# A conv-attention and expert hybrid: one batch's input and the bias tables in the setup, and the order of ScalarE and TensorE in the last passes

## The chip, the cores and the metric

The kernel runs on one core of one Trainium2 chip. A core has TensorE (PE, matrix products into PSUM), VectorE (DVE), ScalarE (ACT), GpSimd (POOL) and SyncE (SP, which here only issues DMAs). Each engine works through its own instruction stream in order, and streams meet at semaphores. The metric is the device time of one execution in microseconds, median of several runs.

## What is computed

The input x has 16 batches of 16 x 48 tokens of 128 channels. Three blocks follow one another, each added to its input:

```python
x = x + conv_attention(group_norm(x))     # 8 heads, softmax over 768 tokens of a batch, two relative-position biases
t = tokens(x)
t = t + additive_attention(layer_norm(t))
#   hidden = tanh(A[:, :, None, :] + B[:, None, :, :]);  logits = hidden . w2;  attn = softmax(logits);  attn @ v
t = t + experts(layer_norm(t))            # softmax gate, top 2 of 8 experts, capacity 1920 rows each,
                                          # gelu(rows @ w1 + b1) @ w2 + b2, weighted and added back
```

The additive attention needs a tanh for every query, key and hidden unit, and the biases of the first attention are gathered from two small tables (95 x 8 and 31 x 8).

## The kernel before

Work is a pipeline over batches with five stages: `pre` (group norm, q, k, v, and q and k split into three bf16 parts), `max` (row maxima of the scores), `mid` (the first attention and what `add` needs), `add` (the tanh attention) and `end` (gate, top 2, and rows sent to the experts). In pass b, `pre` works on batch b + 3, `max` on b + 2, `mid` on b + 1, `add` on b and `end` on b - 1. A pass has 24 ticks, and a tick has four slots. Tables (`AT`, `MAX_COUNTS`) say at which tick a product stands, and every engine writes the same passes in its own stream, so the order is fixed when the program is written.

**The setup.** `passes` (L189 on, in the listing below) starts with pieces of passes: `pre` of batch 0, ticks 0 to 17; then each engine's `prepare`; then `pre` of batch 1, ticks 0 to 17; then batch 0's last `pre` ticks with the first maxima, then `max` of batch 0, and so on. SP loads the x of batch 0, weights and tables, then writes two constant blocks into `q_max` and two into `k_max` (L620 to L624; the latter wait for ScalarE's `setup_act`), stores batch 0's parts (L693) and loads them back for the maxima (`load_max`, which waits for `parts_stored`). Batch 1's x is loaded at the first tick of its pass (L688), into `x_in`. That tile also holds the rest of k of batch 0 while it is split (`qk_rest`, L265). DVE's `prepare` first makes the bias tables: seven small operations that split the table `tn_raw` into three bf16 parts and put them together in `tn_all` (L1141 to L1155), then eight copies that spread it into `bias_q` (L1157). It goes on with transposed weights (L1164 to L1177) and gate constants. ScalarE fills the other 48 partitions of `bias_q` behind that (L858). The first scores of batch 0 (L948) read `bias_q`. GpSimd's `prepare` makes masks and ends with a DMA that clears expert rows (L789).

**The last passes.** Pass 15 is the one with `add` but no `mid`: per tick GpSimd writes three sums into one of four `hidden` slots (L803, 3 instructions), ScalarE takes the tanh of these in place, 128 x 2304 elements, the wide one (L902), then a narrow one for the fourth column straight from `b_rep` (L906); TensorE multiplies the slot by w2 into `logits` (L978, the product of tick t stands in tick t + 1). Every fourth tick a block of 128 queries is complete: DVE takes its maximum (L1447, L1449), ScalarE its exponential (L886, `exp_logits`, at t = 5, 9, 13, 17, 21 ahead of that tick's wide tanh, and for the last block at t = 1 of the next pass), TensorE transposes it and multiplies by v (L1071, L1074), and DVE normalises and adds. The first product of the next block waits for the exponential, since it overwrites `logits`. GpSimd may run four ticks ahead of the products. Pass 16 has `end` alone: the last block, layer norm, gate (L1078), top 2, positions (L1083 to L1094), then twelve row sends by GpSimd (L814).

**The experts.** Ten chunks of 384 rows per pair of experts: transposes (L458), up products (L471), gelu (L510), down products (L482), weights by DVE (L545 to L552), and three scattering DMAs a chunk by GpSimd (L583). The first up product waits for rows, weights and the bias `down_b`.

## Time and profile before

| | |
|---|---|
| median of 3 runs | 2384.56 us (2372.84 to 2385.24) |
| profiled execution, its own time | 2384.78 us |
| its span, first to last instruction | 2383.0 us |
| PE busy | 2053.2 us (86%) |
| DVE, ACT, POOL busy | 1675.7 (70%), 1683.2 (71%), 1461.3 us (61%) |
| mean granted TensorE clock | 0.951 |

Time and span differ by 1.8 us, which lies around the first and last instruction. Busy shares are means over a setup, twelve equal passes in a loop, some unrolled ones and the expert part, so what a stage waits for has to be read from that stage. In the page's 40 slices of 60 us, PE is busy for 2 tenths in the first, and for 7, 7, 5 and 4 tenths in the four slices from 1966 to 2145 us; elsewhere it is at 7 to 9 tenths or more. A granted clock of 1.00 is 2.4 GHz and one of 0.50 is 1.2 GHz.

### The profile page before, as it was taken

The numbers are of one execution on the slowest core, as the hardware profiler recorded it, in microseconds if no ns is written. First come the engines' busy times: TensorE is split into PE (matmuls) and PEld (weight loads), VectorE is DVE, ScalarE is ACT, GpSimd is POOL, SyncE is SP. The second block draws the span as 40 slices with busy tenths as digits, with TensorE's granted clock in tenths as the row PEclk, the third lists the DMA queues.
The fourth block names the chain that finished last, engine by engine and source line by source line (L and its number), as shares of the span: only waits on it lengthen the run. The fifth ranks groups of instructions, "written<-read, shape, count | busy, mean of one in ns | idle before, by whom it ended". The sixth has DMA issues, their size and how long they took to land.

```text
span 2383.0 us, 56242 instructions
## 1 busy us (share of the span) xinstructions
PE 2053.2 (86%) x17665; PEld 1122.5 (47%) x17665; DVE 1675.7 (70%) x4534; ACT 1683.2 (71%) x1933; POOL 1461.3 (61%) x1525
## 2 busy tenths in 40 slices
PE   2889999989998999989998999999999977549986
PEld 1344444444444444444444444444444433338775
DVE  5787787787878787868786878787877665324433
ACT  5238787877887788778787878788878977613332
POOL 3006576656666656565666666666657877627777
PEclk7799999999999999999999999999999988869998
DMA  4546322322222223222323131313131000025553
GB/s 94 89 86 128 95 48 61 55 62 56 61 56 61 56 59 57 58 60 51 66 50 68 42 70 29 81 32 77 32 65 32 12 6 4 7 54 90 84 86 37
DMA packets 157499, 137.99 MB, mean 58 GB/s; under 512 B 24665, under 2 KB 149814, under 8 KB 157104
## 3 DMA queue, kind: packets, MB, share of 16 engines
q1 hardware_dynamic: 119376, 109.87, 22.5%
q0 software_dynamic: 23824, 16.85, 5.2%
q10 hardware_dynamic: 13968, 7.30, 1.2%
q8 instruction: 154, 2.52, 0.5%
q14 instruction: 177, 1.45, 0.2%
HBM read 82.68 MB, written 54.52 MB: 58 GB/s over the span
## 4 chain that ended last, share of the span: by engine, by line
PE 39%; DVE 22%; issue 13%; DVEq 9%; POOL 6%; ACT 4%; POOLq 3%; DMA 2%; SPq 0%; another core or an unknown queue 0%; ACTq 0%
PE logits L978 12%; DVE max_halves L1261 4%; POOL out_dram L583 4%; PE ring L1052 3%; PE av_bank L964 3%; POOLq L802 3%; PE ring L1074 3%; PE ring L1066 3%; PE scores L948 3%; PE scores L951 2%; ACT hidden L902 2%; DVE logit_bias L1447 2%; POOL hidden L803 2%; PE ring L1071 2%; DVEq L1448 2%
## 5 line engine op out<-in xcount | busy, mean ns | idle before, releaser
L803 POOL TENSOR_SCALAR hidden<-b_rep,a_cols 128x768 f32<-128x768 f32 x1152 | 1057.1, 920 | 765.6 <-issue 302.9
L902 ACT ACTIVATE hidden<-hidden 128x2304 f32<-128x2304 f32 x384 | 816.1, 2125 | 16.4 <-POOL hidden L803 16.4
L978 PE MATMUL logits<-hidden,w_shifted 128*32 128x384 f32 x6144 | 591.6, 504 | 65.3 <-ACT hidden L906 30.9
L879 ACT ACTIVATE probs<-scores 128x512 f32<-128x512 f32 (+1 forms) x768 | 391.9, 545 | 325.6 <-PE scores L951 320.9
L1261 DVE TENSOR_REDUCE max_halves<-ring 128x1 f32<-128x384 f32 (+4 forms) x896 | 471.3, 550 | 115.8 <-PE ring L1052 114.2
L906 ACT ACTIVATE hidden<-b_rep,a_cols 128x768 f32<-128x768 f32 x384 | 358.4, 933 | 0.0
L1052 PE MATMUL ring<-k_max,q_max 112*128 112x384 bf16 (+4 forms) x1024 | 296.0, 319 | 34.8 <-DVE max_halves L1261 25.9
L978 PEld LDWEIGHTS logits<-hidden,w_shifted 128*32 128x32 f32 x6144 | 164.0, 110 | 314.9 <-issue 246.7
L948 PE MATMUL scores<-bias_q,onehot_k 112*128 112x512 bf16 (+1 forms) x768 | 276.4, 360 | 4.8 <-ACT probs L879 1.8
L951 PE MATMUL scores<-q_parts,k_parts 98*128 98x256 bf16 (+1 forms) x1536 | 277.3, 262 | 0.0
L814 POOL DMA_INDIRECT expert_rows<-rows,slots x198 | 199.5, 1007 | 64.2 <-issue 32.7
L964 PE MATMUL av_bank<-probs,v_aug 128*32 128x256 f32 (+1 forms) x3072 | 224.8, 364 | 6.3 <-DVE headsT_raw L1433 6.1
L951 PEld LDWEIGHTS scores<-q_parts,k_parts 98*128 98x128 bf16 x1536 | 153.3, 100 | 116.8 <-issue 20.1
L1052 PEld LDWEIGHTS ring<-k_max,q_max 112*128 112x128 bf16 x1024 | 91.0, 99 | 245.2 <-issue 95.0
L886 ACT ACTIVATE probs<-logits,logit_bias 128x768 f32<-128x768 f32 x96 | 86.6, 902 | 132.7 <-DVE logit_bias L1449 127.9
L1074 PE MATMUL ring<-v,probs1T 128*128 128x128 f32 x1152 | 153.2, 284 | 21.8 <-DVE max_halves L1261 13.0
L1074 PEld LDWEIGHTS ring<-v,probs1T 128*128 128x128 f32 x1152 | 139.5, 195 | 41.4 <-DVE max_halves L1261 19.7
L510 ACT ACTIVATE hidden<-scores,eb1T 128x384 f32<-128x384 f32 x80 | 46.2, 581 | 132.2 <-PE scores L471 129.6
L1319 DVE COPY probs1T<-ring 128x384 f32<-128x384 f32 x192 | 102.6, 548 | 34.5 <-PE ring L1071 34.2
L964 PEld LDWEIGHTS av_bank<-probs,v_aug 128*32 128x32 f32 x3072 | 70.3, 109 | 103.8 <-issue 80.8
L482 PEld LDWEIGHTS logits<-probs,hidden 128*128 128x128 f32 x960 | 113.4, 192 | 12.1 <-issue 1.7
L482 PE MATMUL logits<-probs,hidden 128*128 128x128 f32 x960 | 113.7, 275 | 1.6 <-DVE gn_small L552 1.6
(262 smaller groups left out, 2585.8 us busy)
## 6 DMA issues: line engine op xcount, KB each, us to landing
qk_parts<-qk_parts_sb SPq DMA_DIRECT2D x16, 1152.0 KB, 4.7
q_parts<-qk_parts SPq DMA_DIRECT2D x192, 96.0 KB, 3.2
k_parts<-qk_parts SPq DMA_DIRECT2D x192, 96.0 KB, 4.3
q_max<-qk_parts SPq DMA_DIRECT2D x96, 96.0 KB
k_max<-qk_parts SPq DMA_DIRECT2D x96, 96.0 KB
expert_rows<-clear_row ACTq DMA_DIRECT2D x9, 792.0 KB, 5.0
x_in<-in_x_dram SPq DMA_DIRECT2D x96, 64.0 KB
x<-in_x_dram SPq DMA_DIRECT2D x96, 64.0 KB
```

The lines of the kernel that those rows point to most:

```text
L482: last = mm(logits[:, n % 2, P * b_:P * b_ + P], gelu_out[n % 2][:, j, P * b_:P * b_ + P], down_w[r][:, j, :], start=(j == 0), stop=(j == 3))
L803: last = g.tensor_scalar(hidden[:, q % SLOTS, o, :], b_rep[:, side], 1.0, a_cols[:, side, a_col(q, o):a_col(q, o) + 1], ALU.mult, ALU.add)
L879: s.activation(probs0[:, d % 3, 2 * pair:2 * pair + 2, 0:n_], scores[:, pair].rearrange("p (j l) -> p j l", j=2)[:, :, 0:n_], ACT.Exp) \
L902: s.activation(hidden[:, t % SLOTS, 0:3, :], hidden[:, t % SLOTS, 0:3, :], ACT.Tanh)
L906: s.activation(hidden[:, t % SLOTS, 3, :], b_rep[:, side], ACT.Tanh, bias=a_cols[:, side, col:col + 1]).then_inc(tanh_done, 1)
L948: mm(bank[:, :, 0:n_], onehot_k[:], bias_q[:, h:h + 2, q0 - P * kb:q0 - P * kb + n_], start=True, stop=False, skip_group_check=True)
L951: last = mm(bank[:, j, 0:n_], k_parts[0:98, h + j, P * kb:P * kb + P], q_parts[0:98, h + j, q0:q0 + n_], start=False, stop=True, skip_grou ...
L964: last = mm(av_bank[32 * g:32 * g + 32, q0 - lo:q0 - lo + n_], v_aug[:, side, kb, 4 * quad + g, :], probs0[:, d % 3, g, 0:n_], start=(kb = ...
L978: last = mm(logits[32 * g:32 * g + 32, half, 0:HALF], w2_shifted[:, k, :], hidden[:, q % SLOTS, g, HALF * half:HALF * half + HALF], start= ...
L1052: last = mm(bank[:, keys * j:keys * j + keys], q_max[:, h + j, P * qb:P * qb + P], k_max[:, h + j, lo:lo + keys], start=True, stop=True)
L1074: last = mm(bank[:, 0:P], probs1T[:, P * kb:P * kb + P], v1[:, ps.side(stage), kb, :], start=(kb == 0), stop=(kb == TB - 1))
L1261: v.tensor_reduce(max_halves[:, h:h + n_, part], bank[:, 0:n_ * keys].rearrange("p (h k) -> p h k", h=n_), AX.X, ALU.max, negate=True).the ...
```

## The change

- SP loads the x of batch 1 in the setup, behind the weights, once TensorE has finished transposing batch 0's x (`ring_filled` at 2). The rest of k of batch 0 goes to `x2` instead of `x_in`. Batch 0's parts are stored ahead of the two `k_max` copies, which now stand in `copy_tables`.
- The bias tables (split, put together, and the copies into partitions 0 to 63 of `bias_q`) move from DVE's `prepare` to the end of GpSimd's `prepare`, behind its clearing DMA, with a semaphore `bias_made` for ScalarE and TensorE. There are nine small operations instead of seven.
- In pass 15 `exp_logits` stands between the wide and the narrow tanh.
- `keep_warm(n)` issues n products of 112 x 512 bf16 into `scores[:, 0]`, which nobody reads: 3 in each of the 24 ticks of pass 15, and 14, 4, 16 and 90 of them in ticks 3, 7, 8 and 12 of pass 16.
- In pass 16 ScalarE computes one Gelu of one column behind the gate's exponential.

```diff
+WARM_AT = {3: 14, 7: 4, 8: 16, 12: 90}
...
-        qk_rest = [xT[:], x_in[:].rearrange("p b c -> p (b c)")]
+        def qk_rest(w, c):
+            if w == 0:
+                return xT[:]
+            return (x_in if positive(c) else x2)[:].rearrange("p b c -> p (b c)")
...
+            sp.wait_ge(ring_filled, 2)
+            load_x(1)
             sp.wait_ge(made, 3)
             sp.dma_start(q_max[48:96, :, :], hot_t.unsqueeze(1).to_broadcast([48, H, L])).then_inc(copies_in, 16)
             sp.dma_start(q_max[96:112, :, :], hot_n.unsqueeze(1).to_broadcast([16, H, L])).then_inc(copies_in, 16)
-            sp.wait_ge(setup_act, 1)
-            sp.dma_start(k_max[48:96, :, :], ct_wide).then_inc(copies_in, 16)
-            sp.dma_start(k_max[96:112, :, :], cn_wide).then_inc(copies_in, 16)
...
-                        if t == 0 and positive(count := c * 2):
+                        if t == 0 and positive(count := c * 2) and positive(c - 1):
...
                             if not positive(c):
+                                copy_tables()
                                 load_max(c, 0)
...
                 pool.dma_start(cleared[0], clear_source).then_inc(rows_sent, 16)
+                g.tensor_copy(tn_hi, tn_raw)
+                pool.drain()
+                g.tensor_tensor(tn_rest, tn_raw, tn_hi, ALU.subtract)
+                pool.drain()
...
+                g.memset(flag[:, 0:1], 0.0).then_inc(bias_made, 1)
+                for h in range(H):
+                    last = g.tensor_copy(bias_q[0:64, h, :].rearrange("p (b n t) -> p b n t", n=16, t=8),
+                                         tn_all[0:64, :].rearrange("p (w h) -> p w h", h=H)[:, :, h][:, ::-1]
+                                         .rearrange("p (b t) -> p b t", t=8).unsqueeze(2).to_broadcast([64, TB, 16, 8]))
+                last.then_inc(bias_made, 1)
...
-            act.wait_ge(setup_dve, 2)
+            act.wait_ge(bias_made, 1)
...
-                    if ps.has("add") and t >= 5 and t % 4 == 1:
+                    if ps.has("add") and ps.has("mid") and t >= 5 and t % 4 == 1:
                         exp_logits(ps.batch("add"), t // 4 - 1)
...
                         s.activation(hidden[:, t % SLOTS, 0:3, :], hidden[:, t % SLOTS, 0:3, :], ACT.Tanh)
+                        if not ps.has("mid") and t >= 5 and t % 4 == 1:
+                            exp_logits(b, t // 4 - 1)
...
+                        if not ps.has("add"):
+                            s.activation(logit_bias[:, 0:1], ident[:, 0:1], ACT.Gelu)
...
+                    pe.wait_ge(bias_made, 2)
                     pe.wait_ge(setup_act, 2)
...
+            def keep_warm(n):
+                for _ in range(n):
+                    mm(scores[:, 0, :], ones_bf[0:112, :], bias_q[:, 0, 0:512], start=True, stop=True)
...
+                        if slot == 2 and ps.has("add") and not ps.has("mid"):
+                            keep_warm(3)
+                        if slot == 3 and not ps.has("add") and ps.has("end") and not positive(NB - ps.b):
+                            if t in WARM_AT:
+                                keep_warm(WARM_AT[t])
```

DVE's `prepare` loses the matching lines (L1141 to L1160 before), and the waits on `setup_dve` are renumbered.

GpSimd at the end of its setup, before and after. Names in a row are out<-in, with the shape of the output.

```order
L786 MEMSET rows 128x792
L725 MEMSET flag 128x1
L789 DMA expert_rows<-clear_row 128x12x132
L803 TENSOR_SCALAR hidden<-b_rep,a_cols 128x768 x72
```

```order
L801 DMA expert_rows<-clear_row 128x12x132
L802 CAST tn_parts<-hidden 112x384
L804 TENSOR_TENSOR hidden<-hidden,tn_parts 112x384
L806 CAST tn_parts<-hidden 112x384
L808 TENSOR_TENSOR tn_parts<-hidden,tn_parts 112x384
L811 TENSOR_SCALAR tn_parts<-tn_parts,part_mask 112x384 x3
L813 TENSOR_TENSOR tn_parts<-tn_parts 112x384
L815 TENSOR_TENSOR tn_parts<-tn_parts 112x384
L817 MEMSET flag 128x1
L819 COPY bias_q<-tn_parts 64x768 x8
L836 TENSOR_SCALAR hidden<-b_rep,a_cols 128x768 x72
```

Seventeen operations that stood on DVE between the split of batch 0 and the transposed weights now stand behind GpSimd's clearing DMA.

SP's DMAs from the last small weights to the load of batch 0's parts, before and after.

```order
L620 DMA q_max<-k_parts 48x8x768
L621 DMA q_max<-k_parts 16x8x768
L623 DMA k_max<-q_parts 48x6144
L624 DMA k_max<-q_parts 16x6144
L693 DMA qk_parts<-qk_parts_sb 128x2x2304
L640 DMA q_max<-qk_parts 16x4x768 x3
L640 DMA k_max<-qk_parts 16x4x768 x3
L597 DMA x_in<-in_x_dram 128x1x128 x6
```

```order
L603 DMA x_in<-in_x_dram 128x1x128 x6
L628 DMA q_max<-k_parts 48x8x768
L629 DMA q_max<-k_parts 16x8x768
L704 DMA qk_parts<-qk_parts_sb 128x2x2304
L635 DMA k_max<-q_parts 48x6144
L636 DMA k_max<-q_parts 16x6144
L651 DMA q_max<-qk_parts 16x4x768 x3
L651 DMA k_max<-qk_parts 16x4x768 x3
```

The six loads of x move from behind the load of the parts to the front, and the store of the parts moves ahead of the `k_max` copies.

TensorE in pass 16, from the last block to the first expert rows, before and after.

```order
L1074 MATMUL ring<-v,probs1T 128x128 x6
L1037 MATMUL ring<-ident,rows 128x128 x6
L1078 MATMUL ring<-gateT,headsT 128x8 x6
L1083 MATMUL ring<-chosen,before_same 128x48
...
L1094 MATMUL ring<-chosen,ones_bf 128x8 x6
L458 MATMUL av_bank<-ident,xT 128x128 x3
```

```order
L1116 MATMUL ring<-v,probs1T 128x128 x6
L1022 MATMUL scores<-bias_q,ones_bf 128x512 x14
L1079 MATMUL ring<-ident,rows 128x128 x6
L1022 MATMUL scores<-bias_q,ones_bf 128x512 x4
L1120 MATMUL ring<-gateT,headsT 128x8 x6
L1022 MATMUL scores<-bias_q,ones_bf 128x512 x16
L1125 MATMUL ring<-chosen,before_same 128x48
...
L1136 MATMUL ring<-chosen,ones_bf 128x8 x6
L1022 MATMUL scores<-bias_q,ones_bf 128x512 x90
L464 MATMUL av_bank<-ident,xT 128x128 x3
```

The extra products stand in TensorE's stream behind the last block, the transposes, the gate and the positions, the 90 directly ahead of the first expert rows.

## Rows read from the trace of the kernel before

**Rows 1.** Stretches by time: start:end, length, busy us (count) per engine, PEclk, DMA

```profile
40.00:60.00 20.00, 3.91 (x14) 3.07 (x14) 5.55 (x28) 4.33 (x2) 0.00 (x0) 0.50 0.38 84
```

**Rows 2.** Timeline of DVE in the setup: start, us, operation, [idle before <-releaser]

```profile
28.37 0.77 DVE L1142 CAST tn_parts<-hidden 112x384 bf16<-112x384 f32 x1
...
38.85 0.29 DVE L1164 COPY wv1T<-logits 128x128 f32<-128x128 f32 x1
...
54.02 0.56 DVE L1229 COPY xT<-ring 128x384 f32<-128x384 f32 x1 [10.66 <-PE ring L1037]
```

**Rows 3.** Timeline of SP's DMA issues in the setup

```profile
33.12 1.84 SPq L693 DMA_DIRECT2D qk_parts<-qk_parts_sb  x1
...
47.61 3.81 SPq L597 DMA_DIRECT2D x_in<-in_x_dram  x6
```

**Rows 4.** Timeline of DVE where GpSimd works too

```profile
14.55 0.17 DVE L1131 TENSOR_TENSOR ln_small<-ln_small 128x7 f32<-128x7 f32 x1
14.79 1.41 DVE L1133 SCALAR_TENSOR_TENSOR ln_small<-ln_small 128x7 f32<-128x7 f32 x1
...
2004.38 0.81 DVE L1133 SCALAR_TENSOR_TENSOR ln_small<-ln_small 128x7 f32<-128x7 f32 x1
```

**Rows 5.** Timeline of POOL: what its instructions take

```profile
14.72 1.54 POOL L719 TENSOR_SCALAR_AFFINE_SELECT k_parts<-k_parts 48x768 bf16<-48x768 bf16 x1 [0.19 <-issue]
16.45 1.92 POOL L719 TENSOR_SCALAR_AFFINE_SELECT k_parts<-k_parts 16x768 bf16<-16x768 bf16 x1 [0.19 <-issue]
...
29.90 1.26 POOL L789 DMA_DIRECT2D expert_rows<-clear_row  x1 [0.72 <-POOL flag L725]
...
2000.54 13.44 POOL L803 TENSOR_SCALAR hidden<-b_rep,a_cols 128x768 f32<-128x768 f32 x15
```

**Rows 6.** Timeline of PE at the first scores of batch 0

```profile
91.96 0.63 PE L951 MATMUL scores<-q_parts,k_parts 98*128 98x256 bf16 x2
92.39 0.63 PE L948 MATMUL scores<-bias_q,onehot_k 112*128 112x512 bf16 x1
```

**Rows 7.** Timeline of ACT in pass 15, and the page's group of the wide tanh

```profile
1999.49 0.90 ACT L886 ACTIVATE probs<-logits,logit_bias 128x768 f32<-128x768 f32 x1 [1.05 <-DVE logit_bias L1449]
...
2018.07 0.90 ACT L886 ACTIVATE probs<-logits,logit_bias 128x768 f32<-128x768 f32 x1 [6.16 <-DVE logit_bias L1449]
...
2032.09 0.90 ACT L886 ACTIVATE probs<-logits,logit_bias 128x768 f32<-128x768 f32 x1 [1.54 <-DVE logit_bias L1449]
...
2044.68 0.90 ACT L886 ACTIVATE probs<-logits,logit_bias 128x768 f32<-128x768 f32 x1 [0.24 <-DVE logit_bias L1449]
...
L902 ACT ACTIVATE hidden<-hidden 128x2304 f32<-128x2304 f32 x384 | 816.1, 2125 | 16.4 <-POOL hidden L803 16.4
```

**Rows 8.** Timeline of PE from pass 15 to the first expert chunk

```profile
2011.55 2.93 PE L1074 MATMUL ring<-v,probs1T 128*128 128x128 f32 x12 [3.77 <-DVE probs1T L1319]
...
2016.71 1.50 PE L1078 MATMUL ring<-gateT,headsT 128*128 128x8 f32 x12
...
2026.98 1.60 PE L1074 MATMUL ring<-v,probs1T 128*128 128x128 f32 x12 [0.56 <-DVE probs1T L1319]
...
2088.04 1.54 PE L1037 MATMUL ring<-ident,rows 128*128 128x128 f32 x6 [5.71 <-DVE rows L1217]
2090.23 2.73 PE L1078 MATMUL ring<-gateT,headsT 128*128 128x8 f32 x12 [0.65 <-DVE headsT L1291]
...
2121.32 0.90 PE L458 MATMUL av_bank<-ident,xT 128*128 128x128 f32 x3 [22.59 <-DMA xT<-expert_rows]
...
2124.64 2.93 PE L471 MATMUL scores<-probs1T,probs 128*128 128x384 f32 x4 [0.82 <-DMA v<-in_L_ffn_b_dram]
...
2130.57 1.48 PE L471 MATMUL scores<-probs1T,probs 128*128 128x384 f32 x4
```

**Rows 9.** Timeline of DVE at the end of pass 15

```profile
2073.67 0.16 DVE L1321 RECIPROCAL row_scale<-row_sum 128x1 f32<-128x1 f32 x1 [8.81 <-remote]
```

**Rows 10.** Stretches by time in the last passes, columns as in rows 1

```profile
2072.00:2074.00 2.00, 0.00 (x0) 0.00 (x0) 0.26 (x2) 0.00 (x0) 0.00 (x0) 0.65 0.01 0
```

51 lines of the change are left out of this document (24 added, 27 removed).

## The prediction

> **What bounds the kernel now.** I read the 40 slices first, then stretches and the timeline of each engine where a slice is thin. The change touches nothing in the loop over the full passes, which is most of the span, so its worth lies in two places: the first 95 us and the last 400.
>
> In the setup between 40 and 60 us nothing is near busy: PE has 3.91 us of work in 20, DVE 5.55, POOL none, and the granted clock is at its lower level, 0.50 [rows 1]. DVE shows why. It is through with batch 0 at 28.37, spends 10.48 us on the bias tables (28.37 to 38.85), ends its preparation and then sits idle for 10.66 us until PE has transposed the x of batch 1, so that x enters DVE at 54.02 [rows 2]. That x was issued only at 47.61 [rows 3], behind a DMA queue that had waited for the store of batch 0's parts. From 54.02 on the chain goes through DVE and PE without such a gap up to the maxima of batch 0 and the first scores, at about 92 [rows 6], so what starts this chain earlier moves the rest of the kernel.
>
> In pass 15 the longest stream is ScalarE's: 24 ticks of a wide tanh of 2.1 us [rows 7] and a narrow one. It is interrupted at the exponentials, which wait for DVE's maximum of the block: 1.05, 6.16, 1.54 and 0.24 us before four of them, and the fifth is like the fourth [rows 7]. Behind it comes a sequential tail: last block, layer norm, gate, sends, first chunk. There PE runs at the lower level: the same gate product takes 2.73 us where it takes 1.50 elsewhere, the value product 2.93 against 1.60, and an up product pair 2.93 against 1.48 [rows 8].
>
> **The change part by part.**
>
> *DVE's preparation and the early x: 21.1 us.* The tables leave DVE: 10.48 us off its path. The next thing that was late is x. SP reaches the new load at about 21 us, when its small weights are issued; six loads take 3.81 us to issue [rows 3], and PE had them 5.5 us after the first issue (47.61 to 53.10, which is 54.02 less the transposes). So x is there at about 27, while DVE and PE are ready at 32. The idle 10.66 us goes as well, whole. 10.48 + 10.66 = 21.1 us: x enters DVE at 32.9 instead of 54.02. The two `q_max` copies behind the load on SP come 3.8 us later, and the `k_max` copies behind the parts; only the maxima wait for them. The store of the parts moves from 33.12 [rows 3] to 28.5, DVE's end of batch 0; at the 11.7 us that it and what shared the queues took before (33.12 to 44.8) the load of the parts starts at 40.2 and, with 2.8 us of issue and about 5 of landing, is there at 48. The first maximum, at 68.5 before, wants it at 47.4 if all 21.1 us are kept, so this costs 0.5 us at most and nothing if the next term is real.
>
> *GpSimd's tables in DVE's way: +7 us.* The tables now run on GpSimd from 31.2 (29.90 + 1.26 [rows 5]), just when DVE does the group norm of batch 1. A DVE instruction with two operands in SBUF that takes 0.17 us took 1.41 us when a GpSimd selection of 1.54 us had begun 0.07 us before it, and such instructions take 0.81 us in a row under GpSimd's sums, one per sum [rows 4, 5]. So a DVE instruction of this kind waits for the GpSimd instruction under way. GpSimd's price: a sum of 768 elements takes 13.44 / 15 = 0.90 us, a selection of as many 1.54 to 1.92 [rows 5]. The nine small operations have 384 elements, so 0.45 to 0.96 each; at 0.6, with seven drains of 0.19, the table is ready at 31.2 + 6.7 = 37.9. Each of the eight copies reads and writes 768: 0.90 to 1.92; I take 1.1, near the sum, since a copy is plain arithmetic too, but its source is read backwards in steps. DVE reaches its first two-operand instruction 3.1 us after x enters, at 36.1, and has some twelve until the normalised x is out (two of the mean, one of the variance, nine of the root), 0.245 us apart when alone. Two of GpSimd's small operations and eight copies are still to come then, and each lets one DVE instruction through: 2 x (0.6 - 0.25) + 8 x (1.1 - 0.25) = 7.5; I take 7, since a few overlap reads from PSUM. The bounds are nothing, if these copies do not block, and 2 x 0.7 + 8 x (1.92 - 0.25) = 14.8 us. The SBUF page of the Trainium skill ("SBUF — State Buffer", section "Who interferes with whom") states the same as an exclusive lock: a DVE instruction with two SBUF inputs contends with a GpSimd one that reads SBUF, and the second to issue fully blocks. By that rule this part of the change is charged as here, and without it the sum below would be 7 us lower.
>
> The other waits on the tables have room: ScalarE's part of `bias_q` and its constant rows take 11.3 us behind 37.9, and the first scores would come at 92 - 14 = 78.
>
> *The exponential behind the wide tanh: -5.1 us.* The wait now runs beside 2.1 us of tanh (about 2.0 from start to start). Gain per block: the wait, at most 2.0. 1.05 + 2.0 + 1.54 + 0.24 + 0.25 = 5.1. What is queued behind the exponential is the narrow tanh, 0.8 us, which ends when it ended before. The first product of the next block, which waits for the exponential, comes up to 2.0 us later in its tick, and through it GpSimd's sums four ticks on: product 1.5 us, sums 3 x 0.90, a send of 1.0 where there is one, so 5.2 us, against 0.8 + 2 x 2.85 = 6.5 until ScalarE wants them. That holds with 1.3 us to spare. Bounds: 0, if that loop closes, and 5.1 + 4.1 (the rest of the 6.16) if DVE's chain also shortens.
>
> *Fillers in pass 15: -1.4 us.* A product of 512 columns takes 0.43 us at the lower clock level (two halves, 91.96 to 92.39 [rows 6]), so 0.22 at the upper. Three are 0.65 us a tick, less than PE's idle 1.25 before most products. With the clock up, the value product ahead of the longest wait takes 1.6 instead of 2.9 us [rows 8], on the path to the 2018.07 exponential: 1.3, taken as 1.4 with the products around it. Bounds: +3 (five block ends pushed by 0.65) and -3.
>
> *Fillers in pass 16: -1.7 us.* The transposes at 2088.04 go from 1.54 to 0.87 and the gate from 2.73 to 1.50, together 1.9; the four fillers between them, 0.9 us, stand in a gap of 0.65 [rows 8] and give 0.2 back. The 14 (3.0 us at full speed, 6.0 at half) fit in the idle 5.71 ahead of the transposes, about even in the worst case; the 16 (3.5) in the 5.0 ahead of the positions. Nothing warms PE while it waits for the last exponential, so the last block stays at the lower level.
>
> *The 90, and the first chunk: -2.9 us.* They stand in the 22.59 us in which PE waits for rows [rows 8]: 90 x 0.215 = 19.4 us at full speed. PE is then idle for 3.2 us. After idling from 2068.7 the clock was still granted whole until 2072 and fell in the stretch behind it, 0.65 [rows 10], so it should just last. The first up products start with the bias DMA as before, but take 2 x 1.45 less (2.93 to 1.48 [rows 8], for two pairs). The Gelu table, 1.3 us of ScalarE, is off the path too, but gelu kept up anyway: nothing for it. GpSimd's scatters, the bound of the expert part, start 2.9 earlier.
>
> The sum: 2384.8 (the profiled execution, 0.2 above the median) - 21.1 + 7 - 5.1 - 1.4 - 1.7 - 2.9 = 2359.6, **2360 us**.
>
> One piece stays unexplained: 8.81 us in which DVE stands before a reciprocal although its product was done [rows 9]. I leave it in; were it chance, the time falls by up to 8.8 in either kernel, and one run of before was 12 us below the others.
>
> **The rivals.**
>
> *No contention.* GpSimd's copies don't hold DVE up, or are done before it comes. For: DVE's casts and copies beside GpSimd's masks in the setup are not slowed. Against: rows 4. Time: 2359.6 - 7 + 0.5 = 2353.
>
> *Strided reads cost GpSimd more.* A copy takes 1.92 like the dearest selection: contention 14.8, time 2384.8 - 21.1 + 14.8 - 11.1 = 2367. For: the source steps by 16 bytes. "GPSIMD Engine Reference" of the Trainium skill, section "Performance pitfalls for Q7 kernels", has a rule for custom kernels that reads with more than 8 bytes a step cost half as much again; 1.35 a copy would be an estimate from it, and 2362.
>
> *The 90 fillers become the wait.* If PE does not come to full speed under them they take 90 x 0.43 = 38.7 us, 16 more than the gap of 22.6. The rows come through with PE late, the up products start some 15 later, and terms of the fillers are lost: 2384.8 - 21.1 + 7 - 5.1 + 15 = 2381. Against: dense up products brought the clock up within 6 us at 2124 to 2131 [rows 8]. If it rises after that time, the loss is only about 3.
>
> *Slower than before.* GpSimd's broadcast copy, reversed and in steps, is far dearer than any row shows. It decides at the eight copies in the setup: each costs DVE D - 0.25, and the other terms with the small operations give 31.5, so the point is D = 4.2 us a copy. At 5 us: 2384.8 - 31.5 + 38 = 2391. No row comes to half of that.
>
> *The tail does not move.* The block ends turn out to wait on something that follows along (GpSimd's sums or DVE's chain), and only the setup pays: 2384.8 - 14.1 = 2371.
>
> **How the numbers follow.** Chances: forecast 0.48 (2352 to 2366 around it), no contention 0.16, strided reads 0.13, the tail does not move 0.10, fillers late 0.08, slower 0.05. A measurement of this kernel can tell about 0.5% from no change, 12 us. Faster by over 0.5% (below 2372.6) are the forecast, the first two rivals and 0.06 of the tail case: 0.83. Within 0.5% are the rest of the tail case and the late fillers: 0.12. Slower: 0.05. The unexplained 8.8 us is no case of its own and only widens the lower end. For 8 in 10 the range reaches from 2345 (no contention and half of the 8.8) to 2375.
>
> **What the profile would show.** x of batch 1 enters DVE at about 33 and the first scores come at 78; DVE's small two-operand instructions between 36 and 47 last about as long as GpSimd's copies; GpSimd's copies take 0.9 to 1.9 us; no wait above 0.1 before the exponentials but the second; PEclk 1.00 through pass 15; the 90 fillers end before the rows arrive, and the first up products take 1.5 a pair. Wrong would be a first score before 73 or after 84, a copy above 2 us, a new wait of ScalarE for sums, or PE still in fillers when the rows are there.

## The result and the profile after

The changed kernel takes 2396.11 us (median of 16 runs, 2383.59 to 2406.66), the kernel before 2384.65 us (16 runs of the same set). The ratio is 1.0052 with a 95% interval of 1.0032 to 1.0071: 12 us slower, where the prediction had 25 us faster. By the rule that sorts runs into fast and slow, one run of e5 below (3305.97 us at a granted clock of 0.555) and six of the 13 of e1 (2398.34 to 2412.35 us, clocks of 0.940 to 0.949) are slow; without those six e1's median is 2387.05 us, so e1 alone is weak evidence. The profiled execution took 2394.67 us, its span is 2392.9 us and its mean granted clock 0.955.

The edit of the setup did what it was for. x of batch 1 enters VectorE at 33.62 us instead of 54.02 [rows 2], and the first scores start at 75.25 instead of 91.58. VectorE and TensorE of the changed kernel, timeline (start, us, engine, line, operation, [idle before <-releaser]):

```profile
33.62 0.56 DVE L1255 COPY xT<-ring 128x384 f32<-128x384 f32 x1 [0.17 <-PE ring L1079]
...
75.25 0.59 PE L986 MATMUL scores<-bias_q,onehot_k 112*128 112x512 bf16 x1 [1.51 <-DMA q_parts<-max_parts]
```

To see where this gain goes, one needs a mark that stands once in every pass. The A and B products of a batch (`map_b`) serve. The first of batch 0 and of batch 15, two rows of the kernel before and then two of the changed one, timeline of TensorE:

```profile
179.22 0.91 PE L1066 MATMUL ring<-headsT,map_b 128*128 128x384 f32 x2 [0.65 <-DVE headsT L1291]
1969.13 1.65 PE L1066 MATMUL ring<-headsT,map_b 128*128 128x384 f32 x2 [0.65 <-DVE headsT L1291]
```

```profile
162.78 1.65 PE L1108 MATMUL ring<-headsT,map_b 128*128 128x384 f32 x2 [0.65 <-DVE headsT L1317]
1981.51 2.29 PE L1108 MATMUL ring<-headsT,map_b 128*128 128x384 f32 x3 [0.65 <-DVE headsT L1317]
```

The change is 16.4 us ahead at batch 0 and 12.4 us behind at batch 15. So 28.8 us are lost in between, where no line was edited. From batch 15's mark to the first up product it is 155.4 us (1981.51 to 2136.95) against 155.5 before, and from there to the end 256.0 against 258.4.

The loss is spread over the passes. The stretch from batch 2's mark to batch 14's, kernel before and then changed kernel (columns as in rows 1):

```profile
403.40:1866.50 1463.10, 1333.56 (x12163) 688.37 (x12163) 1145.16 (x3010) 1167.13 (x1309) 945.54 (x1012) 0.98 0.26 55
```

```profile
394.00:1879.30 1485.30, 1346.70 (x12163) 694.37 (x12163) 1153.45 (x3010) 1167.51 (x1309) 948.26 (x1011) 0.97 0.26 54
```

The same 12163 products take 13 us more of TensorE, at a mean granted clock that is a hundredth lower; ScalarE's time is unchanged. Twelve passes became 22.2 us longer. So 13 of the 22 us are TensorE's own time, and the other 9 are time in which it waits. The clock falls to 0.50 for some 3 to 10 us at a time, and there are more such falls in the changed kernel.

### The profile page after: what moved, and what is told of

It is laid out like the page before. It is cut to its first block, busy times and chain, and to the rows that moved or that the text cites. A ratio compares the mean times of both kernels' runs of the same rounds, so it can differ in the third digit from the quotient of the medians.

```text
span 2392.9 us, 56635 instructions
## 1 busy us (share of the span) xinstructions
PE 2110.4 (88%) x17861; PEld 1146.6 (48%) x17861; DVE 1686.9 (70%) x4517; ACT 1684.0 (70%) x1934; POOL 1486.8 (62%) x1543
## 4 chain that ended last, share of the span: by engine, by line
PE 37%; DVE 22%; issue 14%; DVEq 10%; POOL 7%; POOLq 5%; ACT 3%; DMA 2%; SPq 1%; ACTq 0%
PE logits L1016 11%; DVE max_halves L1287 4%; POOLq L835 4%; POOL out_dram L589 4%; PE ring L1116 3%; PE ring L1094 3%; PE av_bank L1002 3%; PE ring L1108 3%; POOL hidden L836 2%; PE scores L986 2%; PE scores L989 2%; DVE logit_bias L1473 2%; ACT hidden L935 1%; PE ring L1113 1%; PE ring L1090 1%
## 5 line engine op out<-in xcount | busy, mean ns | idle before, releaser
L1094 PEld LDWEIGHTS ring<-k_max,q_max 112*128 112x128 bf16 x1024 | 91.0, 99 | 257.4 <-issue 93.0
```

The lines of the kernel that those rows point to most:

```text
L1094: last = mm(bank[:, keys * j:keys * j + keys], q_max[:, h + j, P * qb:P * qb + P], k_max[:, h + j, lo:lo + keys], start=True, stop=True)
```

## The experiments

All ran with 5 rounds. A ratio is to the kernel before on the same chip, whose median was 2382.75 us beside e1 to e4, 2388.36 beside e5 to e8, 2384.93 beside e9 to e12 and 2382.72 beside e13 to e16; so medians of different groups can't be compared, and ratios can. 0.001 is 2.4 us. An interval of one ratio is 0.002 to 0.004 to each side, so a difference of two ratios is uncertain by 7 to 10 us. The recorded ratios differ from the quotients of the medians by up to 0.002, most in e8, where the quotient is 1.0031. "Start" below is the number of instructions of an engine's stream ahead of the loop over pairs of passes, waits, drains and register instructions counted, as the built program has them. "mod 128" is the remainder of that number after division by 128, and a drain is an instruction that computes nothing; the kernel sets it between dependent ones. The table holds every run; the last column counts falls of the clock that begin 74 to 83 us behind a mark, for the marks of batches 1 to 12 in the profiled execution.

| kernel | median us | ratio [95%] | VectorE start (mod 128) | GpSimd start (mod 128) | falls at 74 to 83 us |
|---|---|---|---|---|---|
| before | 2384.65 | 1 | 786 (18) | 269 (13) | 0 |
| the change | 2396.11 | 1.0052 [1.0032, 1.0071] | 761 (121) | 294 (38) | 4 |
| e1 setup only | 2396.00 | 1.0059 [1.0030, 1.0088] | 761 (121) | 294 (38) | 2 |
| e2 tail only | 2384.35 | 1.0004 [0.9975, 1.0034] | 786 (18) | 269 (13) | 0 |
| e3 x early only | 2370.78 | 0.9937 [0.9906, 0.9968] | 786 (18) | 269 (13) | 0 |
| e4 tables only | 2412.11 | 1.0109 [1.0072, 1.0146] | 761 (121) | 294 (38) | 4 |
| e5 setup, VectorE + 25 | 2393.54 | 1.0021 [0.9990, 1.0051] | 786 (18) | 294 (38) | 0 |
| e6 x early, GpSimd + 25 | 2388.59 | 0.9996 [0.9970, 1.0023] | 786 (18) | 294 (38) | 0 |
| e7 x early, VectorE + 103 | 2393.82 | 1.0022 [0.9996, 1.0048] | 889 (121) | 269 (13) | 5 |
| e8 change, VectorE + 25 | 2395.73 | 1.0013 [0.9989, 1.0038] | 786 (18) | 294 (38) | 0 |
| e9 setup, both aligned | 2373.44 | 0.9954 [0.9930, 0.9978] | 786 (18) | 397 (13) | 0 |
| e10 change, both aligned | 2374.41 | 0.9952 [0.9925, 0.9980] | 786 (18) | 397 (13) | 0 |
| e11 x early again | 2368.93 | 0.9943 [0.9913, 0.9972] | 786 (18) | 269 (13) | 0 |
| e12 x early and tail | 2371.87 | 0.9949 [0.9922, 0.9975] | 786 (18) | 269 (13) | 0 |
| e13 x early, VectorE + 128 | 2381.42 | 0.9985 [0.9966, 1.0004] | 914 (18) | 269 (13) | 0 |
| e14 x early, VectorE + 64 | 2382.28 | 0.9994 [0.9973, 1.0015] | 850 (82) | 269 (13) | 0 |
| e15 x early, GpSimd + 64 | 2383.93 | 1.0005 [0.9981, 1.0029] | 786 (18) | 333 (77) | 0 |
| e16 x early, VectorE + 32 | 2373.95 | 0.9958 [0.9935, 0.9980] | 818 (50) | 269 (13) | 0 |

### Which part: the change taken to pieces

**Setup alone (e1)**: the changed kernel without the tail edits.

```diff
-WARM_AT = {3: 14, 7: 4, 8: 16, 12: 90}
-                        if slot == 2 and ps.has("add") and not ps.has("mid"):
-                            keep_warm(3)
...
-                    if ps.has("add") and ps.has("mid") and t >= 5 and t % 4 == 1:
+                    if ps.has("add") and t >= 5 and t % 4 == 1:
```

> The change without its last passes: no filler products, exponentials ahead of the wide tanh again, no Gelu in pass 16; x early and tables on GpSimd stay. In the profile of the change the first scores come 16.3 us earlier (75.25 against 91.58), but the first product of the last A/B step of the loop's successor, batch 15's, comes 12.4 us later (1981.5 against 1969.1), so 29 us go in the full passes. Theory A (something in the setup edit slows the full passes): about as slow as the change, 2394 to 2400, with passes of 124 us. Theory B (the tail edits do it, by what they add to the engines' code behind the loop): back to about 2384.6 - 16 = 2368.

**Tail alone (e2)**: the kernel before with the moved exponential, the fillers and the Gelu.

```diff
+WARM_AT = {3: 14, 7: 4, 8: 16, 12: 90}
+                        if slot == 2 and ps.has("add") and not ps.has("mid"):
+                            keep_warm(3)
```

> The kernel before with the edits of the last passes alone (fillers, exponential behind the wide tanh, Gelu). Theory A: full passes as before, so 2384.6 less what the tail gives, 0 to -3 by the profile of the change (from batch 15's first A/B product to the first up product it takes 155.4 us against 155.5; the expert part is 2.4 shorter): 2382 to 2385. Theory B: full passes 27 us longer, about 2410. By the prediction's sum the tail gives 11: 2374.

**The early x alone (e3)**: e1 with the table code back in VectorE's `prepare`.

```diff
             def prepare():
+                dve.wait_ge(made, 2)
+                v.tensor_copy(tn_hi, tn_raw)
...
-                g.tensor_copy(tn_hi, tn_raw)
...
```

> The setup edit without the move of the tables: x of batch 1 early, parts stored ahead of the k_max copies, bias tables on VectorE as before, tail as before. The first scores should come 10.7 us earlier, at 81. If the move to GpSimd slows the full passes (theory A1), their length is as before (121.8 us a pass) and the time 2374. If the early x or the order of DMAs does it (theory A2), or an earlier start as such, 2384.6 - 11 + 27 = 2401.

**The tables on GpSimd alone (e4)**: the kernel before with the table code moved, x loaded late.

```diff
-                v.tensor_copy(tn_hi, tn_raw)
...
+                g.tensor_copy(tn_hi, tn_raw)
...
```

> The kernel before with the bias tables on GpSimd alone; x of batch 1 loaded late as before. The setup gains nothing or a little, since x bounds it (0 to 2 us). Theory A1 (the tables on GpSimd slow the full passes): 2384.6 + 27 = 2412. Theory A2 (x early or the order of DMAs): 2384.

The setup edit makes the loss (e1 1.0059 for 1.0052), and the tail edits nothing that can be told (e2 1.0004). Within the setup, the early x is worth 12 to 15 us (0.9937), and moving the tables to GpSimd costs 26 to 29 us: 1.0109 against 1, and 1.0059 against 0.9937. This cost does not arise in the setup. In e1 the first mark stands at 160.9 us, in e3 at 169.4, so the move of the tables *gains* 8.5 us there. It is lost in passes that the tables have no part in.

### Why tables in the setup slow a loop that doesn't touch them

What the move changes for the loop is where its instructions stand. The table code is 25 instructions with waits and drains, so VectorE's loop starts 25 earlier, at 761, and GpSimd's 25 later, at 294. Theory C was that this position matters on VectorE, rival P the same on GpSimd, rival M anything else that GpSimd's table work might bring.

VectorE's timeline shows it. A few instructions of the loop are held for a time that no semaphore explains, and in one kernel they are the same ones in every trip. In the kernel before there are two (each comes back every second pass):

```profile
473.42 0.56 DVE L1296 TENSOR_TENSOR x<-ring,x 128x384 f32<-128x384 f32 x1 [0.36 <-issue]
531.96 0.55 DVE L1304 TENSOR_REDUCE a_cols<-xnT 128x48 f32<-128x384 f32 x1 [0.45 <-issue]
```

In the changed kernel there are three:

```profile
468.82 0.69 DVE L1287 TENSOR_REDUCE max_halves<-ring 128x1 f32<-128x512 f32 x1 [0.26 <-issue]
496.40 1.86 DVE L1374 TENSOR_TENSOR qk_parts_sb<-x_in,qk_parts_sb 128x384 bf16<-128x384 f32 x2 [0.45 <-issue]
590.96 0.21 DVE L1400 TENSOR_TENSOR rt<-rt,rs 128x48 f32<-128x48 f32 x1 [0.38 <-issue]
```

Counted through the built program, before they are instructions 1474 and 1729, after 1473, 1601 and 962. Modulo 128 all five are 65 or 66. The profile's list of DMA queues has instruction traffic; kernel before, then changed kernel (queue, kind, packets, MB, share):

```profile
q14 instruction: 177, 1.45, 0.2%
```

```profile
q14 instruction: 182, 1.49, 0.2%
```

1.45 MB / 177 = 8.2 KB a packet, which over 128 instructions is 64 bytes each. The number of packets follows the position too. Between a start of 294 and the end of its 416 instructions GpSimd's loop holds four places that are 66 modulo 128, the edges of such a grid (322, 450, 578 and 706), and from 269, 333 or 397 it holds three. Over six trips through the loop that would be six packets more. The list has 182 or 183 packets in the six kernels with GpSimd's start at 294, and 177 or 178 in eleven others; e14, whose VectorE start leaves out one edge, has 173. That q14 serves these two engines is inferred from this and not shown by name. The other instruction queue, q8, moved 154 or 155 packets of 16.4 KB in every kernel.

"Runtime: NRT & Kernel Launch" of the Trainium skill, section "Instruction fetch mechanics", says that an engine streams its instructions in blocks and hides nearly all of their cost, but gives a block as 256 instructions. The stalls here stand on a grid of 128, and 0.22 to 0.47 us of one are not hidden where the engine isn't waiting anyway.

**VectorE's position put back (e5, e8).** Drains just before the loop, in e5 to the kernel of e1, in e8 to the whole change:

```diff
-    def passes(eng, body, prepare=None):
+    def passes(eng, body, prepare=None, pad=0):
...
+        for _ in range(pad):
+            eng.drain()
         with eng.Fori(0, (last_full - first_full + 1) // 2) as two:
...
-            passes(dve, body, prepare)
+            passes(dve, body, prepare, pad=25)
```

> The setup edit without the tail edits (as in the run setup_only, 2396.0 us), with 25 drains added on VectorE just before the loop over pairs of passes: as many instructions as the table code took with it to GpSimd, so that VectorE's loop starts at instruction 786 again, as before, while GpSimd's stays 25 later (294 for 269). Theory C, VectorE's code position: the stalls of 0.38 us of VectorE at its 962nd instruction (in the choice of the two best experts, 73 us behind the A and B products) and of 0.45 us at its 1601st go back to the 1474th and 1729th, the dips of TensorE's granted clock 75 to 81 us behind those products are gone, and the time is that of x_early_only, 2371 us (2366 to 2377). Rival P, GpSimd's code position or its new kinds of instruction: 2396 us, dips at 75 to 81 us still there. Rival M, some other effect of the tables on GpSimd: 2396 us as well.

> The whole change with 25 drains on VectorE just before the loop over pairs of passes. Theory C: VectorE's loop stands where it stood before, and the change gives what its setup gives, 2369 us (2360 to 2376), the tail edits about 0 as in the run tail_only; it beats both kernels. Rivals P and M: 2396 us, no change from the changed kernel.

Neither the expected 2371 nor 2396. The ratios fell by 0.0038 and 0.0039, 9 us each, which is no more than the uncertainty of either difference (by the medians of e8 it would be 5 us). The falls of the clock at 74 to 83 us went from 2 and 4 to none. So part of the loss is VectorE's position, and part is something else.

**GpSimd's position alone (e6)**: e3, no table work on GpSimd, with 25 drains there.

```diff
-            passes(pool, body, prepare)
+            passes(pool, body, prepare, pad=25)
```

> The x edit alone (tables on VectorE, 2370.8 us) with 25 drains added on GpSimd just before the loop over pairs of passes, so that GpSimd's loop starts at instruction 294 as in the change, and VectorE's at 786 as before. No new kind of GpSimd instruction. Theory C (VectorE's code position): 2371 us (2366 to 2377), no dips of the clock 75 to 81 us behind the A and B products. Rival P (GpSimd's code position): 2396 us with those dips.

0.9996 for 0.9940 (mean of e3 and e11): 13 us, with nothing but 25 drains ahead of GpSimd's loop. Theory C alone is refuted, and rival P alone too, since there are no falls at 74 to 83 us here.

**VectorE's position alone (e7)**: e3 with 103 drains on VectorE, which puts its loop at 889, 128 behind the change's 761.

```diff
-            passes(dve, body, prepare)
+            passes(dve, body, prepare, pad=103)
```

> The x edit alone (tables on VectorE, 2370.8 us) with 103 drains added on VectorE just before the loop over pairs of passes: its loop starts at instruction 889, which is 128 behind the 761 of the change. If the stalls come every 128 instructions, they land on the same two instructions of the loop as in the change (the second mask of the best expert, and the first two-operand subtraction of the parts of q and k). Theory C: 2396 us (2388 to 2402), of it at most some 6 us for the drains themselves; the dips 75 to 81 us behind the A and B products appear although the tables are on VectorE. Rival P and rival M: 2371 to 2377 us, no such dips.

1.0022. The stalls came exactly where they stand in the change, with the tables on VectorE. The one in the choice of the two best experts (L1392, the change's L1400) and what follows, timeline of VectorE and TensorE in e7 (batch 3's pass), and then the granted clock in stretches of 2 us (column before the last two):

```profile
592.57 0.21 DVE L1392 TENSOR_TENSOR rt<-rt,rs 128x48 f32<-128x48 f32 x1 [0.38 <-issue]
592.86 0.75 DVE L1394 TENSOR_TENSOR rt<-rt,tie_rank 128x48 f32<-128x48 f32 x1
...
594.45 0.81 DVE L1402 TENSOR_TENSOR rt<-tie_rank,rs 128x48 f32<-128x48 f32 x1
...
596.66 0.78 DVE L1394 TENSOR_TENSOR rt<-rt,tie_rank 128x48 f32<-128x48 f32 x1
```

```profile
596.06 0.39 PE L1070 MATMUL ring<-k_max,q_max 112*128 112x512 bf16 x1 [1.09 <-DVE probs1T L1337]
598.10 2.29 PE L1092 MATMUL ring<-v,probs1T 128*128 128x128 f32 x9 [1.29 <-DVE max_halves L1279]
```

```profile
594.00:596.00 2.00, 0.97 (x8) 0.53 (x8) 1.76 (x5) 2.00 (x4) 1.54 (x2) 1.00 0.00 0
596.00:598.00 2.00, 0.74 (x9) 0.25 (x9) 1.76 (x5) 2.00 (x2) 1.22 (x2) 0.82 0.00 0
598.00:600.00 2.00, 1.90 (x9) 1.91 (x10) 1.76 (x6) 0.23 (x1) 0.00 (x0) 0.50 0.00 0
```

Behind the stall of 0.38 us the chain that chooses the two best experts runs in step with GpSimd's sums: small instructions that take 0.21 us alone take 0.75 to 0.81, as in rows 4. TensorE waits 1.09 and then 1.29 us for VectorE, is busy for 0.97 and 0.74 us in two stretches of 2 us, and its clock falls to 0.50. Over all kernels: with VectorE's start at 121 (mod 128) this fall occurs in 15 of 48 passes, all 15 among the 24 passes of the loop's half that has the stall; with any other start in 0 of 168. That the stall makes the step is read from these counts.

**Both positions put back (e9, e10)**: 25 drains on VectorE as in e5, and 103 on GpSimd at the end of its table code, where it waits anyway, in e9 to the kernel of e1, in e10 to the whole change.

```diff
                 last.then_inc(bias_made, 1)
+                for _ in range(103):
+                    pool.drain()
```

> The setup edit without the tail edits, with 25 drains on VectorE before its loop (start at 786, as before) and 103 drains on GpSimd behind the tables, where it waits anyway (start at 397, which is 128 behind the 269 of the kernel before). Theory C2, that the position of both engines' loops against a boundary every 128 instructions makes the loss in the full passes: both stand as before, so the ratio to the kernel before is that of the x edit alone or better (0.9937; 0.990 to 0.996), the dips of TensorE's clock in passes 3 to 13 last some 45 to 60 us in all, and passes 3 to 13 take 1345 to 1360 us in the profiled execution. Rival N, the tables on GpSimd themselves (new kinds of instruction there, or the time at which the first passes start): ratio 1.002, as with VectorE's 25 alone, 75 to 85 us of dips, 1365 to 1372 us.

> The whole change with both paddings. Theory C2: ratio 0.9937 (0.988 to 0.997), below both kernels. Rival N: 1.001 to 1.005.

0.9954 and 0.9952. The whole change with 128 drains more does the same work, with the tables on GpSimd, and is 22 to 24 us faster than the change as it was given. Rival N, GpSimd's table work as such, is refuted. As given, 1.0052; with VectorE at its old position 1.0013 (-9 us); with GpSimd too 0.9952 (-15 us).

**The reference of these verdicts, once more (e11), and with the tail (e12)**: e11 is e3 again, and e12 is e3 with the tail edits.

```diff
+WARM_AT = {3: 14, 7: 4, 8: 16, 12: 90}
...
+                        if not ps.has("mid") and t >= 5 and t % 4 == 1:
+                            exp_logits(b, t // 4 - 1)
```

> The x edit alone once more, since the verdicts on the paddings rest on its 0.9937 from another set of runs. If that stands: 0.991 to 0.9965. If it was a good draw: 0.998 to 1.000, and GpSimd's 25 drains (0.9996) had no effect.

> The x edit with the tables on VectorE, and the tail edits: neither moves a loop's start. Sum of the two alone (0.9937 and 1.0004): 0.994, and it beats both kernels. If the tail edits cost something that the run tail_only hid, 0.996 to 1.000.

Both as expected, 0.9943 and 0.9949. The early x alone, e3 and e11, is the fastest kernel found and beats both given ones, and the tail edits add nothing to it.

**Position or count (e13 to e16)**: e3 with 128 drains on VectorE before the loop (e13), with 64 (e14) and with 32 (e16), and with 64 on GpSimd (e15).

```diff
-            passes(dve, body, prepare)
+            passes(dve, body, prepare, pad=128)
```

> The x edit alone (0.9937 and 0.9943 in two sets of runs) with 128 drains on VectorE just before the loop: a whole period of the supposed boundary, so the loop's instructions stand against it as in the x edit, but with 25 more drains than the run dve_shifted had. Theory C2 (position): 0.991 to 0.9965, the stalls of VectorE at the 688th and 943rd instruction of its loop, no dips of the clock 75 to 81 us behind the A and B products. Rival D (the drains themselves, or their delay of the first loop pass, cost the 20 us that dve_shifted showed): 1.002 to 1.005.

> The x edit alone with 64 drains on VectorE before the loop: half a period. Theory C2: the stalls move to other instructions (to the 624th and 879th of the loop, or where the engine isn't waiting anyway), and the ratio is anywhere from 0.988 to 1.003, since nothing says that the places of before are the best ones. Rival D: 0.998 to 1.000, half of what 103 drains cost.

> The x edit alone with 64 drains on GpSimd before the loop (start at 333). Theory C2 for GpSimd: the first sum of each trip of the loop, 0.9 us later with 25 drains, and the row DMA that stalled 0.31 us stand elsewhere; ratio from 0.990 to 1.002. Rival D on GpSimd (the drains cost): at least what 25 cost, 0.9996 or more.

> The x edit alone with 32 drains on VectorE before the loop. Theory C2: the stalls at the loop's 656th and 911th instruction or hidden; 0.988 to 1.003. Rival D: 0.996 to 0.998, a third of what 103 cost. With the runs of 0, 64, 103 and 128 drains this gives the cost by position: a curve that falls back at 128 for theory C2, one that rises with the count for rival D.

With 0, 32, 64, 103 and 128 drains on VectorE the ratio is 0.9940, 0.9958, 0.9994, 1.0022 and 0.9985. It falls by 0.0037 from 103 to 128, although 25 drains were added, so it is position; but it does not fall back all the way, so the drains cost too. They can be seen once, ahead of the loop, as a time in which VectorE waits for nothing; e13, timeline of VectorE:

```profile
296.59 0.42 DVE L1451 COPY headsT_raw<-av_bank 128x256 f32<-128x256 f32 x1 [5.86 <-issue]
```

With 32, 64, 103 and 128 drains this idle time is 1.51, 3.33, 5.03 and 5.86 us. From batch 1's mark to batch 2's it is 129.3 us in e14, 128.4 in e7 and 127.1 in e13, and 119.7 to 125.5 in the other fifteen. The idle time is about half of e13's 11 us and a quarter of e14's 13; the rest of both was not traced. Of e7's 20 us, e13's 11 come with the drains and 9 (e7 less e13, 0.0037) with the position, the same 9 that e5 and e8 gave. Each of the three differences is about as large as its uncertainty, and together they put VectorE's share at 9 us, give or take 5. The stalls of VectorE follow the grid in each: instructions 1602 and 1857 in e13, 1090 and 1601 in e14, 962, 1345 and 1730 in e16.

GpSimd at 333 is as bad as at 294 (e15 1.0005). On GpSimd only the starts that are 13 modulo 128 (269 and 397) were good, and the kernel before stood there by luck. Why 333 is bad was not settled. Nor did any run put a whole 128 drains right ahead of GpSimd's loop, as e13 did on VectorE: in e9 and e10 the 103 stand earlier, behind the tables. That the drains of e6 and e15 do harm by delaying GpSimd, and not by moving its loop, is therefore less well excluded than for VectorE; against it stands that 25 drains cost 13 us and 64 only 16.

### GpSimd's instructions next to VectorE's, and TensorE's clock

The commonest fall of the clock stands at the mark itself. Ahead of it VectorE normalises three blocks into `heads`, which TensorE waits for. The same three instructions in two kernels, with the sum of GpSimd next to them; e11, timeline of GpSimd, VectorE and TensorE ahead of batch 4's mark at 635.62:

```profile
630.93 0.91 POOL L815 TENSOR_SCALAR hidden<-b_rep,a_cols 128x768 f32<-128x768 f32 x1 [0.17 <-issue]
...
631.45 0.97 DVE L1233 TENSOR_SCALAR heads<-x,ln_mv,ln_small 128x128 f32<-128x128 f32 x3
...
632.55 0.54 PE L1053 MATMUL ring<-ident,heads 128*128 128x128 f32 x3 [0.51 <-DVE heads L1233]
```

And e8, ahead of batch 4's mark at 643.01, with the clock behind it:

```profile
637.25 1.01 POOL L849 DMA_INDIRECT expert_rows<-rows,slots  x1 [0.15 <-issue]
637.52 2.29 DVE L1245 TENSOR_SCALAR heads<-x,ln_mv,ln_small 128x128 f32<-128x128 f32 x3
...
638.29 0.93 POOL L838 TENSOR_SCALAR hidden<-b_rep,a_cols 128x768 f32<-128x768 f32 x1
...
639.94 0.54 PE L1081 MATMUL ring<-ident,heads 128*128 128x128 f32 x3 [2.11 <-DVE heads L1245]
```

```profile
638.00:640.00 2.00, 0.06 (x1) 0.06 (x2) 2.00 (x4) 0.48 (x1) 1.19 (x2) 1.00 0.13 38
640.00:642.00 2.00, 1.53 (x14) 0.71 (x14) 1.62 (x6) 0.02 (x1) 1.23 (x2) 1.00 0.00 0
642.00:644.00 2.00, 0.99 (x2) 0.65 (x3) 0.88 (x2) 2.00 (x3) 1.80 (x3) 0.67 0.03 6
644.00:646.00 2.00, 2.00 (x7) 0.95 (x5) 0.62 (x1) 2.00 (x3) 0.70 (x1) 0.50 0.26 75
```

In e8 a row-sending DMA of GpSimd is under way when the three begin, and a sum follows it at once. The three then take 2.29 us instead of 0.97, TensorE waits 2.11 us instead of 0.51, is busy for 0.06 us in 2, and its clock falls. In e11 the sum comes first and the row send behind it, and the three are hardly held. "SBUF — State Buffer" of the Trainium skill, section "Who interferes with whom", counts a VectorE instruction of this kind among those that may share a port pair with GpSimd, where one blocks the other whole. The trace agrees in so far as the first of e8's three ends only when GpSimd's sum has ended, at 639.22.

Over all 18 profiled executions and the marks of batches 2 to 13, the three took over 1.6 us together in 98 cases, and the clock fell behind 95 of these; in the other 118 cases, of at most 1.48 us, it fell in 28. In 83 of the 98 long cases a row send was under way when the three began and a sum followed it; this was so in none of the other 118. So what decides is the order of GpSimd's instructions at that moment. With both starts as before (modulo 128), 45 of 96 were long; with GpSimd's moved alone, 32 of 48. But in the change, e1 and e4, where both starts are moved, only 10 of 36 were long. More such cases are thus a path by which e5, e6, e8 and e15 can lose time; for the change itself the count does not show it.

What the position changes on GpSimd itself is small. With its start at 294 (the change, e1, e4, e5, e6 and e8) a row-sending DMA, the 455th instruction and five behind an edge of the grid at 450, waits 0.31 to 0.33 us instead of 0.15; the changed kernel, timeline of GpSimd:

```profile
618.97 1.01 POOL L847 DMA_INDIRECT expert_rows<-rows,slots  x1 [0.32 <-issue]
```

The first sum of each trip through the loop comes 0.9 us later there as well: the shortest gap ahead of it is 2.35 to 2.42 us in the change, e5 and e6, and 1.45 to 1.52 in before, e3, e9 and e11. Neither shift can be the whole cause: in e15, with the start at 333, no row send waits 0.31 us and the shortest gap is 1.47, and yet it is as slow as e6. How GpSimd's position leads to the loss stays open.

**What a fall costs.** Take the time of the 11 passes from batch 2's mark to batch 13's and the total length of the falls in them, counted in stretches of 2 us. The extremes are e16 with 34 us of falls and 1343.3 us, e11 with 37 and 1345.0, e13 with 78 and 1370.5, and e8 with 85 and 1372.3; before has 48 and 1347.3, the change 78 and 1368.8. A line through all 18 is 1327 + 0.52 x falls, with a correlation of 0.94. That is what one would expect if a microsecond at half clock costs half a microsecond. A correlation doesn't say which comes first, though: the waits that bring the clock down also lengthen a pass themselves. By this line the 30 us more of falls in the change are 16 of its 21 us, which fits the 13 us that TensorE's own time grew by. One profile of a kernel is one draw, though. e1's profiled execution had only 41 us of falls and took 2361.99 us, 34 below its kernel's median of 2396.0.

## Why the prediction was wrong

The prediction was 2360 us, 36 below the 2396 measured. Here it is taken apart with the ratios above (differences of them, each uncertain by some 8 us):

- **"The change touches nothing in the loop over the full passes."** This step failed, and it is 24 of the 36 us (1.0052 to 0.9952). The edit moved 25 instructions from one stream to the other ahead of the loop; with VectorE's start put back the kernel is 9 us faster, and with GpSimd's too another 15. The prediction priced the instructions that moved, and not what stands behind them. All rivals shared this step. The one that was slower than before came to 2391 us by copies of 5 us each, and a copy took 1.54.
- **Early x and VectorE's preparation, -21.1.** Right in size: x 20.4 us earlier. The test "x enters DVE at about 33" held (33.62), and the first scores came at 75.25 for a forecast of 78, inside its bounds of 73 and 84. Of the 14.1 us that it left after contention, 11 arrive (e9, 0.9954).
- **GpSimd's tables in VectorE's way, +7.** Wrong in place. The small instructions of the norm took 0.16 to 0.22 us each, without any contention, since GpSimd was not there. Its timeline in the changed kernel:

```profile
30.51 0.51 POOL L802 CAST tn_parts<-hidden 112x384 bf16<-112x384 f32 x1
43.22 0.91 POOL L804 TENSOR_TENSOR hidden<-hidden,tn_parts 112x384 f32<-112x384 f32 x1 [12.20 <-issue]
...
46.02 4.05 POOL L811 TENSOR_SCALAR tn_parts<-tn_parts,part_mask 112x384 bf16<-112x384 bf16 x3 [0.20 <-issue]
...
52.45 12.28 POOL L819 COPY bias_q<-tn_parts 64x768 bf16<-64x768 bf16 x8
```

  Between its first and second instruction GpSimd stood for 12.20 us without a wait (4.23 in e4, where x comes late; why was not found). The table was ready at 52.4 instead of 37.9, and the small operations and the copies met a later part of VectorE's work. The two subtractions of the parts of k took 3.45 us, where they took 1.19 in the kernel before:

```profile
52.76 3.45 DVE L1374 TENSOR_TENSOR qk_parts_sb<-x_in,qk_parts_sb 128x384 bf16<-128x384 f32 x2
```

  From x entering VectorE to the first scores it is 41.6 us in the change and 37.6 in the kernel before, so some 4 us were lost where 7 were charged. A copy took 12.28 / 8 = 1.54 us, inside the forecast's 0.90 to 1.92 and above the 1.1 taken.
- **The exponential behind the wide tanh, -5.1.** The longest wait stayed, as said, but it varies too much to show a gain: 4.2 to 13.1 us in the thirteen kernels without the edit and 3.7 to 10.4 in the five with it. The next wait, 1.54 before, is still 1.13, though the tanh now stands ahead of it, and the one behind that grew from 0.24 to 1.59:

```profile
2036.35 0.90 ACT L919 ACTIVATE probs<-logits,logit_bias 128x768 f32<-128x768 f32 x1 [10.11 <-DVE logit_bias L1475]
2049.96 0.90 ACT L919 ACTIVATE probs<-logits,logit_bias 128x768 f32<-128x768 f32 x1 [1.13 <-DVE logit_bias L1475]
```

  The block's end follows along, which is what the rival "the tail does not move" said.
- **Fillers, -1.4, -1.7 and -2.9.** They raised the clock only in part, and it bought nothing. In pass 15 the forecast was a clock of 1.00 throughout, and it still was 0.50 from 2014 to 2018 and from 2028 to 2032. In pass 16 they worked: before, 44 us at half clock end with the first up products; with the fillers the mean clock from 2098 to 2130 us was 0.99. But the interval from batch 15's mark to the first up product is 149.9 to 162.0 us in the five kernels with the tail edits, and 147.1 to 162.9 in the other thirteen. What stands in it are waits for the last block, the gate and the rows, in which TensorE is not late. The 90 ended before the rows came, as expected, and then:

```profile
2111.66 19.59 PE L1022 MATMUL scores<-bias_q,ones_bf 112*128 112x512 bf16 x90
2134.53 0.55 PE L464 MATMUL av_bank<-ident,xT 128*128 128x128 f32 x3 [3.29 <-DMA xT<-expert_rows]
...
2136.95 2.71 PE L477 MATMUL scores<-probs1T,probs 128*128 128x384 f32 x4 [0.30 <-DMA v<-in_L_ffn_b_dram]
2139.49 1.45 PE L477 MATMUL ring<-probs1T,probs 128*128 128x384 f32 x4
```

  After 3.29 us idle the clock fell once more, and the first pair of up products took 2.71 us where 1.5 was forecast. The prediction had reasoned from a row that the clock "should just last"; it did not. From the first up product to the end, 256.0 to 257.4 us with the edits and 256.6 to 258.4 without.
- **All tail edits together, -11.1.** Five comparisons, with one set of positions in each: e2 with before +0.0004, the change with e1 -0.0007, e8 with e5 -0.0008, e10 with e9 -0.0002, e12 with the mean of e3 and e11 +0.0009. Their mean is -0.0001, with some 4 us of uncertainty to each side, against the 11.1 forecast. This is 11 of the 36 us, and the rival "the tail does not move" was right about it.
- **The 8.81 us that stayed unexplained** [rows 9] have no answering row in the change, nor did the time fall by them. Nine of the eighteen executions have such a stand before this reciprocal, of 5.7 to 8.8 us, and nine have none.

24 + 11 + 3 for the setup are 38 us for the 36 that were missing, which agrees within what the ratios can tell. The forecast's own path in the setup was sound; its largest error is the term for the loop, put at nothing.

What stays open: how GpSimd's position or delay leads to the 15 us, why it is bad at 333 too, and which instruction of its loop matters; why the 8.5 us that the tables on GpSimd gain at the first mark are not in the time of e9 against e3 (0.9954 and 0.9940); and what sets the length of the longest exponential wait.

## What to carry to other kernels

Code that moves between engines ahead of a loop also moves the loop's place in each instruction stream. In this kernel that was worth up to 1% of the time, as much as the edit itself. So compare such a change with a version whose loops start at the same place modulo 128, padded with drains where the engine waits anyway, before the edit is judged. When a loop that was not edited gets slower, set a mark in each pass, sum the falls of the granted clock between marks, and look at what TensorE waited for just ahead of each fall. Raising the clock of an engine in a stretch where it is not the one waited for bought nothing here.

## What the runs showed of the hardware

- VectorE stalls of 0.22 to 0.47 us stand on a grid of 128 instructions. Six starts of its loop (761, 786, 818, 850, 889 and 914) showed them at ten places, all 65 or 66 modulo 128, and the instruction queue q14 moves 8.2 KB a packet.
- Three VectorE instructions of 128x128 f32 take 0.97 us at the end of a 128x768 sum of GpSimd (e11), and 1.9 to 2.3 us when a row-sending DMA of GpSimd is under way as they begin and a sum follows (83 cases). Where they took over 1.6 us, TensorE's clock fell right behind in 95 of 98 cases.
- GpSimd stood 12.20 us between its first cast and its first two-operand instruction, with no semaphore between them (11.8 to 12.9 in six kernels with the early x, 4.23 in e4).
- 32, 64, 103 and 128 drains in a row on VectorE took 1.51, 3.33, 5.03 and 5.86 us (e16, e14, e7, e13).
